# Seven weight tiles in the ring, two places of source rows and an output taken in halves: a change to the first attention of a two-layer graph network

## The reference

```python
# layer 0
x_l = (x @ W + b).reshape(N, 8, 64)
alpha_l = einsum('nhc,hc->nh', x_l, att_l); alpha_r = einsum('nhc,hc->nh', x_l, att_r)
scores = where(adj > 0, alpha_l[:, None, :] * alpha_r[None, :, :], -9e15)
att = softmax(scores, axis=1)
x = layernorm(x + relu(einsum('ijh,jhc->ihc', att, x_l)))
# layer 1: scaled dot attention, queries x, keys x2, values v, the same mask
x = layernorm(x + attention(q=x, k=x2, v=v, adj))
```

## Time and profile before

| | us |
|---|---|
| median of 3 runs | 3721.69 (3721.36 to 3723.89) |
| the profiled execution, its own time | 3723.63 |
| span of that execution in the trace | 3721.7 |
| TensorE busy | 3514.0 (94%) |
| VectorE busy | 2925.2 (79%) |
| ScalarE busy | 2527.6 (68%) |
| GpSimd busy | 1535.2 (41%) |
| mean granted TensorE clock | 0.955 |

### The profile page before, as it was taken

One profiled execution on the slowest core, in us unless ns is written; L12 is line 12 of the kernel. 1 busy time (PEld: TensorE's weight loads), 2 busy tenths in 40 slices (PEclk: granted clock), 3 DMA queues, 4 the chain that ended last, 5 costly groups with the idle time before them and its releaser, 6 DMA issues. The chain is left out here.

```text
span 3721.7 us, 57866 instructions
## 1 busy us (share of the span) xinstructions
PE 3514.0 (94%) x22311; PEld 1411.8 (38%) x22311; DVE 2925.2 (79%) x2984; ACT 2527.6 (68%) x2430; POOL 1535.2 (41%) x1154
## 2 busy tenths in 40 slices
PE   6886999999999999987699999999999999999987
PEld 4554222222222222235244444444444444444434
DVE  6666999999999999977577777777777777777768
ACT  4555999999999999953466566666666666666642
POOL 2222011011011011010277776777766667766761
PEclk9988999999999999985799999999999999999995
DMA  8987677777767777667799999999999999999987
GB/s 282 312 303 252 154 155 158 155 157 167 162 156 157 158 155 165 149 162 244 174 200 198 203 205 201 203 203 199 202 205 204 200 199 201 204 204 201 196 188 246
DMA packets 370652, 729.38 MB, mean 196 GB/s; under 512 B 26672, under 2 KB 215088, under 8 KB 354016
## 3 DMA queue, kind: packets, MB, share of 16 engines
q0 software_dynamic: 99408, 419.90, 58.1%
q1 hardware_dynamic: 236944, 272.23, 23.8%
q10 hardware_dynamic: 34048, 33.82, 2.7%
HBM read 263.50 MB, written 59.69 MB: 87 GB/s over the span
## 5 line engine op out<-in xcount | busy, mean ns | idle before, releaser
L1131 DVE TENSOR_TENSOR a_weights<-a_psS,maskT 128x1024 f32<-128x1024 f32 x1024 | 1206.0, 1220 | 465.5 <-ACT a_psS L1095 465.4
L1095 ACT ACTIVATE a_psS<-a_psS,shift_bc 128x1024 f32<-128x1024 f32 x1024 | 1071.4, 1084 | 678.8 <-PE a_psS L1023 678.7
L541 DVE TENSOR_TENSOR g_weights<-g_weights,maskT 128x1024 f32<-128x1024 f32 x1024 | 1169.8, 1219 | 116.6 <-ACT g_weights L528 116.6
L528 ACT ACTIVATE g_weights<-al_bc,shift_bc,g_xl 128x1024 f32<-128x1024 f32 x1024 | 1167.9, 1228 | 88.0 <-PE g_psD L566 88.0
L1023 PE MATMUL a_psS<-a_q,a_k 128*64 128x512 f16 x8192 | 971.3, 380 | 18.9 <-DMA a_k<-k_scratch 17.2
L1040 PE MATMUL a_psO<-a_weights,a_v 128*64 128x512 f32 x4096 | 961.2, 592 | 0.0
L557 PE MATMUL g_psO<-g_weights,g_xl 128*64 128x512 f32 x4096 | 923.6, 598 | 14.3 <-DVE g_weights L541 14.3
L1154 POOL TENSOR_TENSOR a_pool_total<-a_pool_total,a_weights 128x1024 f32<-128x1024 f32 x336 | 924.8, 2753 | 0.0
L1023 PEld LDWEIGHTS a_psS<-a_q,a_k 128*64 128x64 f16 x8192 | 463.3, 110 | 648.7 <-issue 318.9
L1162 POOL DMA_DIRECT2D a_dma_total<-a_weights x480 | 466.2, 971 | 398.8 <-DVE a_weights L1131 207.8
L557 PEld LDWEIGHTS g_psO<-g_weights,g_xl 128*64 128x64 f32 x4096 | 277.8, 137 | 651.2 <-issue 521.6
(11 more groups left out here) (122 smaller groups left out, 1373.2 us busy)
## 6 DMA issues: line engine op xcount, KB each, us to landing
a_dma_total<-a_weights POOLq DMA_DIRECT2D x512, 512.0 KB, 5.4
g_total<-g_weights POOLq DMA_DIRECT2D x128, 1024.0 KB, 7.8
adj_sb<-in_adj_dram SPq DMA_DIRECT2D x128, 512.0 KB, 6.0
g_xl<-xl_scratch SPq DMA_DIRECT2D x128, 260.0 KB, 5.6
a_k<-k_scratch SPq DMA_DIRECT2D x256, 128.0 KB, 5.4
a_v<-in_L_gnn_v_dram SPq DMA_DIRECT2D x128, 256.0 KB, 4.0
al_bc<-alpha_scratch SPq DMA_DIRECT2D x16, 1024.0 KB, 7.1
f_oT<-o_scratch SPq DMA_DIRECT2D x16, 1024.0 KB, 7.5
```

Of the source, the lines that this page charges most:

```text
L528: nc.scalar.activation(w[:, u % RING, h, :], al_bc[:, g % 2, h, :], ACT.Exp, bias=shift_bc[:, 0, g % PAIRS * 2 + h:g % PAIRS * 2 + h + 1], ...
L541: nc.vector.tensor_tensor(w[:, u % RING, h, :], w[:, u % RING, h, :], maskT[:, j, (g // PAIRS) * IC:(g // PAIRS + 1) * IC], ALU.mult).then ...
L1095: nc.scalar.activation(psS[n % RING][:], psS[n % RING][:], ACT.Exp, bias=shift_bc[:, 1, g % PAIRS * 2 + h:g % PAIRS * 2 + h + 1], scale=SC ...
L1131: nc.vector.tensor_tensor(w[:, u % NP, h, :], psS[n % RING][:].rearrange("p a c -> p (a c)"), maskT[:, j, (g // PAIRS) * IC:(g // PAIRS + ...
```

## The change

The ring gets a seventh place, the source rows lose their third, and `o_sb` holds half of the output. TensorE's denominators come in runs of three. The output is taken and stored in two halves, the first behind tile 4 and the second behind tile 8 of the next group; `taken` counts three and `stored` 64 to a group. In the row stages the query buffers get a third place, `normalize` handles one tile per step, from four steps behind the first tile of its round, the last round is stored tile by tile, and the fp32 product that turns the denominators is issued as a transpose.

```diff
-        RING = 6
-        XS = 3
+        RING = 7
+        XS = 2
-        COUPLES = {2: (0, 2), 4: (3, 4), 7: (6, 7)}
+        RUNS = {3: (0, 2, 3), 7: (4, 6, 7)}
-        o_sb = sb("g_o", [P, IC], F32)
+        o_sb = sb("g_o", [P, HALF], F32)
...
             def store(g):
                 ic, pair = g // PAIRS, g % PAIRS
-                sp.wait_ge(taken, 2 * g + 2)
-                sp.dma_start(o_dram[0, pair, :, ic * IC:(ic + 1) * IC], o_sb[:]).then_inc(stored, 16)
+                for hf in range(2):
+                    sp.wait_ge(taken, 3 * g + hf + 1)
+                    sp.dma_start(o_dram[0, pair, :, ic * IC + hf * HALF:ic * IC + (hf + 1) * HALF], o_sb[:]
+                                 ).then_inc(stored, 16)
+                sp.wait_ge(taken, 3 * g + 3)
                 for hf in range(2):
                     sp.dma_start(d_dram[...], d_sb[32 * hf:P:64, :]).then_inc(stored, 16)
...
-            def take(g):
-                act.wait_ge(closed, g + 1)
-                if g > 0:
-                    act.wait_ge(stored, 48 * g)
-                nc.scalar.activation(o_sb[:], psO[g % 2][:].rearrange("p a c -> p (a c)"), ACT.Copy).then_inc(taken, 1)
-                nc.scalar.activation(d_sb[:], psD[g % 2][:], ACT.Copy).then_inc(taken, 1)
+            def take(g, hf):
+                if hf == 0:
+                    act.wait_ge(closed, g + 1)
+                if hf == 1 or g > 0:
+                    act.wait_ge(stored, 64 * g + 16 * hf)
+                nc.scalar.activation(o_sb[:], psO[g % 2][:, hf, :], ACT.Copy).then_inc(taken, 1)
+                if hf == 1:
+                    nc.scalar.activation(d_sb[:], psD[g % 2][:], ACT.Copy).then_inc(taken, 1)
...
-                if j == 4 and g > 0:
-                    take(g - 1)
-            take(GROUPS - 1)
+                if j in (4, 8) and g > 0:
+                    take(g - 1, j // 4 - 1)
+            for hf in range(2):
+                take(GROUPS - 1, hf)
...
-                if j % JB in COUPLES:
-                    for t in COUPLES[j % JB]:
+                if j % JB in RUNS:
+                    for t in RUNS[j % JB]:
```

and in `finish_layer`:

```diff
+        QB = 3
-            qh = sb("qh", [P, 2, PAIRS, 2 * P], F16)
-            ql = sb("ql", [P, 2, PAIRS, 2 * P], F16)
+            qh = sb("qh", [P, QB, PAIRS, 2 * P], F16)
+            ql = sb("ql", [P, QB, PAIRS, 2 * P], F16)
...
-        STEPS = NT + LAG if first else NT + 1
+        STEPS = NT + LAG if first else NT + T
...
-                nc.tensor.matmul(psR[t % 2][:], dT[0:H, par, cols], identF[0:H, 0:H], start=True, stop=False)
+                nc.tensor.matmul(psR[t % 2][:], dT[0:H, par, cols], identF[0:H, 0:H], is_transpose=True, start=True,
+                                 stop=False, skip_group_check=True)
...
-            def normalize(r):
-                act.wait_ge(rstd_ready, r + 1)
-                act.wait_ge(offset_ready, r + 1)
-                for s in range(T):
-                    nc.scalar.activation(z[...], z[...], ACT.Identity, bias=..., scale=...).then_inc(res_ready, 1)
-                act.wait_ge(res_ready, T * (r + 1))
-                act.dma_start(result[r * T * P:(r + 1) * T * P, :]...).then_inc(res_stored[r % ZB], 16)
+            def normalize(t):
+                r, s = divmod(t, T)
+                if s == 0:
+                    act.wait_ge(rstd_ready, r + 1)
+                    act.wait_ge(offset_ready, r + 1)
+                nc.scalar.activation(z[...], z[...], ACT.Identity, bias=..., scale=...).then_inc(res_ready, 1)
+                if r == R - 1:
+                    act.wait_ge(res_ready, t + 1)
+                    act.dma_start(result[t * P:(t + 1) * P, :], z[:, r % ZB, s, :]).then_inc(res_stored[r % ZB], 16)
+                elif s == T - 1:
+                    act.wait_ge(res_ready, t + 1)
+                    act.dma_start(result[r * T * P:(r + 1) * T * P, :]...).then_inc(res_stored[r % ZB], 16)
...
-                if t > 0 and t % T == 0 and t <= NT:
-                    normalize(t // T - 1)
+                if T <= t < NT + T:
+                    normalize(t - T)
```

More of the change, by code:

```diff
@@ L462, in summed_by @@
         def summed_by(u):
-            return u // JB * len(COUPLES) + sum(j < u % JB for j in COUPLES) + 1
+            return u // JB * len(RUNS) + sum(j < u % JB for j in RUNS) + 1
         def added_by(u):
@@ L501, in _ @@
             store(GROUPS - 1)
-            sp.wait_ge(stored, 48 * GROUPS)
+            sp.wait_ge(stored, 64 * GROUPS)
         @block.scalar
         def _(act):
-            def take(g):
-                act.wait_ge(closed, g + 1)
-                if g > 0:
-                    act.wait_ge(stored, 48 * g)
-                nc.scalar.activation(o_sb[:], psO[g % 2][:].rearrange("p a c -> p (a c)"), ACT.Copy).then_inc(taken, 1)
-                nc.scalar.activation(d_sb[:], psD[g % 2][:], ACT.Copy).then_inc(taken, 1)
+            def take(g, hf):
[6 more added lines that the diff above has]
+                    nc.scalar.activation(d_sb[:], psD[g % 2][:], ACT.Copy).then_inc(taken, 1)
             for u in range(GROUPS * NT):
@@ L550, in values @@
                 if j == 0 and g >= 2:
-                    pe.wait_ge(taken, 2 * (g - 1))
+                    pe.wait_ge(taken, 3 * (g - 1))
                 if u % KB == 0:
@@ L680, in finish_layer @@
             v_loaded = sem("v_loaded")
-            q_stored = [sem(f"q_stored{i}") for i in range(2)]
+            q_stored = [sem(f"q_stored{i}") for i in range(QB)]
             tail = sem("tail")
         block = ctx.enter_context(nc.Block())
-        STEPS = NT + LAG if first else NT + 1
+        STEPS = NT + LAG if first else NT + T
         @block.sync
@@ L729, in turn @@
                     pe.wait_ge(inverted, t - 1)
-                nc.tensor.matmul(psR[t % 2][:], dT[0:H, par, cols], identF[0:H, 0:H], start=True, stop=False)
-                nc.tensor.matmul(psR[t % 2][:], alone[:, par, cols], times_n[:], start=False, stop=True
-                                 ).then_inc(turned, 1)
+                nc.tensor.matmul(psR[t % 2][:], dT[0:H, par, cols], identF[0:H, 0:H], is_transpose=True, start=True,
+                                 stop=False, skip_group_check=True)
+                nc.tensor.matmul(psR[t % 2][:], alone[:, par, cols], times_n[:], start=False, stop=True,
+                                 skip_group_check=True).then_inc(turned, 1)
             def turn_queries(t):
@@ L760, in deviations @@
                 nc.scalar.activation(std[:, r % 2, :], mv[:, r % 2, :, 1], ACT.Sqrt, bias=eps[:]).then_inc(std_ready, 1)
-            def normalize(r):
-                act.wait_ge(rstd_ready, r + 1)
-                act.wait_ge(offset_ready, r + 1)
-                for s in range(T):
-                    nc.scalar.activation(z[:, r % ZB, s, :], z[:, r % ZB, s, :], ACT.Identity,
-                                         bias=offset[:, r % 2, s:s + 1], scale=rstd[:, r % 2, s:s + 1]
-                                         ).then_inc(res_ready, 1)
-                act.wait_ge(res_ready, T * (r + 1))
-                act.dma_start(result[r * T * P:(r + 1) * T * P, :].rearrange("(t p) c -> p t c", p=P),
-                              z[:, r % ZB, :, :]).then_inc(res_stored[r % ZB], 16)
+            def normalize(t):
[3 more added lines that the diff above has]
+                    act.wait_ge(offset_ready, r + 1)
+                nc.scalar.activation(z[:, r % ZB, s, :], z[:, r % ZB, s, :], ACT.Identity,
+                                     bias=offset[:, r % 2, s:s + 1], scale=rstd[:, r % 2, s:s + 1]
+                                     ).then_inc(res_ready, 1)
+                if r == R - 1:
[3 more added lines that the diff above has]
+                    act.wait_ge(res_ready, t + 1)
+                    act.dma_start(result[r * T * P:(r + 1) * T * P, :].rearrange("(t p) c -> p t c", p=P),
+                                  z[:, r % ZB, :, :]).then_inc(res_stored[r % ZB], 16)
             def upper(t):
@@ L775, in upper @@
                 act.wait_ge(q_turned, t + 1)
-                if half == 0 and pair >= 2:
-                    act.wait_ge(q_stored[pair % 2], 32 * (pair // 2))
-                nc.scalar.activation(qh[:, pair % 2, :, half * P:(half + 1) * P], psQ[t % 3][:], ACT.Copy
+                if half == 0 and pair >= QB:
+                    act.wait_ge(q_stored[pair % QB], 32 * (pair // QB))
+                nc.scalar.activation(qh[:, pair % QB, :, half * P:(half + 1) * P], psQ[t % 3][:], ACT.Copy
                                      ).then_inc(qh_ready, 1)
@@ L784, in store_queries @@
                     act.dma_start(q_dram[part].rearrange("(a p) n -> p a n", p=P)[:, :, pair * 2 * P:(pair + 1) * 2 * P],
[L785 removed]
+                                  qq[:, pair % QB, :, :]).then_inc(q_stored[pair % QB], 16)
             act.wait_ge(consts_set, 1)
             for t in range(STEPS):
[L789 to L790 removed]
+                if T <= t < NT + T:
+                    normalize(t - T)
```

(12 more changed lines are left out.)

## The result

The changed kernel takes 3784.23 us (median of 5 runs, 3776.70 to 3784.61) against 3722.01 before; the ratio is 1.0162, with an interval of 1.0148 to 1.0176. It is 62 us slower; 3775 was forecast, in a range of 3745 to 3830. The spans of the two profiled executions are 3782.7 and 3721.7 us.

A forecast was written before the change was run, and what follows sets the result against it. TensorE was taken to set the first attention's pace, while no engine fills the row stage. Terms -18.6 + 78 + 10 + 3 - 18.9 gave +53.5 on 3723.6 us, so 3777, put at 3775; range 3745 to 3830.

The forecast's parts named there:

- the forecast's own case: Whole kernel: the first half's store makes TensorE wait, with five clock falls; 3755 to 3795 us, 56% chance.
- four switches in place of six: First attention, TensorE: runs of three save 0.29 us per 8 tiles, 64 times, -18.6 us.
- wait for the first half's store: First attention: ScalarE waits for the store before tile 9, TensorE idles; 5.2 us in each of 15 groups, +78 us.
- clock behind the waits: TensorE after its idles: five of 15 waits bring half clock, about 2 us each, +10 us.
- end of the stage: End of first attention: the first half's landing is exposed, less a shorter first copy, +3 us.
- first row stage: Row stage behind the first attention: shorter VectorE waits, third query place, shorter tail and transpose; -18.6 us.
- second row stage: Last row stage: VectorE waits for nothing the change moves, end costs 0, transpose saves some 0.3 us.
- The count: SyncE, first attention: load_xl(g, 3) now waits for tile 7, not tile 3; the store behind it leaves at 17.3 us.
- The rival that it falls every time: First attention: TensorE's clock falls in every group, costing 45 us in place of 10; 3810 us, 22% chance.
- The ring: First attention: seven places suffice for the runs of three, with 1.7 us to spare; cost 0.
- Source rows: First attention: two places cost 0 unless loads take over 7.1 us; up to 20 us more, that rival 10%.
- The signs: Expected trace: 15 ScalarE waits of 5 to 6 us, 15 TensorE idles of about 4, stage at 1340 to 1350.

The follow-up runs named there:

- e1: Changed kernel with store(g-1) one block earlier, behind load_xl(g, 2) in place of load_xl(g, 3); 3685.03 us, ratio to before 0.9895.
- e3: Changed kernel with 64 filler matmuls behind tile 8's matmuls in groups 1 to 15, where TensorE otherwise idles; 3768.84 us, ratio 1.0123.
- e6: e1 with the old couples of denominators in place of the runs of three; 3747.63 us, ratio 1.0064.
- e5: Kernel before with only the runs of three, keeping six ring places, three places of source rows and whole output; 3819.83 us, ratio 1.0258.
- e9: Kernel before with two places of source rows in place of three, nothing else; 3760.53 us, ratio 1.0095.
- e10: e1 with the last group's second half put into the idle tile total, so ScalarE takes it without waiting; 3684.39 us, ratio 0.9892.
- e2: Changed kernel with the store left where it is, but the second half taken behind tile 12 in place of tile 8; 3684.79 us, ratio 0.9898.

## Why the prediction was right

The time lies in the forecast's own case, 9 us above its 3775, and the mechanism that was to decide it, the wait for the first half's store, is the one that the runs show. The clock behaved as a rival had it, and not as the forecast's own case did; that this changed the sum by only 4 us is luck. In us, forecast and shown:

| term | forecast | shown | by |
|---|---|---|---|
| four switches in place of six | -18.6 | -18.5 | e1 against before: 79.85 - 78.70, 16 times |
| wait for the first half's store | +78 | +84 | e3 against e1: 5.58, 15 times |
| clock behind the waits | +10 | +14 | after against e3: 0.95, 15 times |
| end of the stage | +3 | +1.5 | last `total` to next load, 7.45 against 6.00 |
| first row stage | -18.6 | -20.2 | from there to the second attention's load, 133.07 against 153.29 |
| second row stage | -0.3 | -0.8 | from its first load to the end of the span, 101.9 against 102.7 |

They add up to 60 us; the spans differ by 61. The forecast had 53.5: the wait and the clock took 10 us more than their terms, and the other four together gave 3.5 us more than theirs. The first row is the difference of the whole first attention without the wait; that the switches make it is read from the blocks (9.73 us, as worked out), since the run that changed them alone (e6) brought other waits with it.

- *The count.* That `load_xl(g, 3)` waits for tile 7 and the store stands behind it was read off the code, and SyncE's row confirms it to a tenth of a us (17.3). Two edits, each at one end of the wait, take away all of it. This is shown.
- *The wait's size.* The landing was taken as 3.3 us from rows of other stages and is 3.7 on average; the idle was to be 4.0 us and is 3.9 to 4.9, once 6.05. The 0.4 us of landing are what a group was short (5.2 forecast, 5.58 shown), and more than half of them come from the three stores that land late (ScalarE's longest wait is 8.2 us).
- *The clock.* Here two errors met, and they nearly cancelled by luck. I took five falls of 2 us each; there were 15, of 0.95 us on average. The rival that it falls every time was right in its count and wrong in its price of 3 us: behind the wait TensorE runs at ScalarE's 2.27 us a tile anyway, and half clock (about 3.4 us a tile, twice 1.71) costs only the difference, for one or two tiles. By the rule of the Trainium skill that I weighed ("TensorE: Matmul & The Clock Gate", section "HAM oscillation — how this bites in real kernels"), a recurring wait brings the half clock back each time; the trace agrees, 15 times of 15.
- *The ring.* A cost of 0, with 1.7 us to spare, held (e1), and the same reckoning gave that six places would not do, which e5 bears out; but it left out some 0.4 us between the last denominators and the next tile's mask, and so e5's loss came out a third too small.
- *Source rows.* Zero was right, but for a reason that I did not see. I feared loads of 5.6 us and up to 9.4; with the runs of three their median is 2.9, and the longest in the changed kernel's stage takes 5.3. They are issued well away from the accumulating DMAs (see the last section). With the couples some take 6.9 to 9.3, and there two places do lose time (e6, e9).
- *End of the stage.* I took the landing of 3.3 us, less 0.4. With no load ahead of it the first half landed in 2.1 us here (1725.91 to 1728.02), and it left 0.9 us sooner than the whole store did before (1.74 us behind the last `total` matmuls in place of 2.64). So 1.5 us are left, and e10's trace is without them.
- *Row stages.* The six waits of 2.4 us went. From the first to the last of VectorE's waits for the square root, six rounds apart, 16.8 us were won (98.83 before, 82.01 after) where 15.8 were forecast; the tail behind them gave 3.0 for 2.5. Where the one us more in the rounds comes from is open.
- *The signs.* The new wait, the 15 idles, the blocks of 7.0 and 2.7 us and the row stage came as named; ScalarE's waits were 6.4 us and not 5 to 6, and the stage took 1359 us and not 1340 to 1350.

## What to carry to other kernels

When a buffer is halved and taken in two steps, the store between them can join the path: look at what stands ahead of it on its queue, and at the count that this waits for, since a smaller ring elsewhere (here XS) shifts that count. Look also at when the second half is taken. In e1, one `kb == 2` in place of `kb == 3` turned 62 us lost into 39 won, and in e2 a later take did the same. The third place of source rows could be given up here only together with the order of work in which the loads land early.

## What the hardware showed that I had not expected

- A load of 260 KB takes 6.7 to 9.3 us to land when it is issued 0.4 to 1.8 us behind an accumulating DMA of 1 MB: so did all 61 such loads of the kernel before, 22 in e6 and 20 in e9. The others, issued 6 us or more behind one or less than 0.3 us behind it, land in 2.7 to 5.0 us in the same three kernels. In e1 and in the changed kernel every load of the stage is issued 6 us or more behind one, and lands in 2.7 to 5.3 us. The kernel before has the most late loads and waits for none of them: that is what its third place was for. That the distance to the accumulating DMA is the cause is read from the times of both queues; no run moved a load by itself.
- TensorE's clock was at 1.2 GHz behind each of 15 idles of 3.9 to 6.1 us, and at 2.4 GHz throughout the stage where short matmuls filled them (e3). A fall cost only 0.95 us on average here, since ScalarE and not TensorE sets the pace behind the wait.
